# GpSimd's clearing between scatters: 8 columns in place of 384, and behind more of the scatters

## The reference

```
x = x + layernorm(linear_attention(layernorm(x)))     # 16 heads of 8, scan over the 256 rows
x = x + layernorm(moe(layernorm(x)))

moe(x) = shared(x) + sum over the two best of 8 experts of gate_e(x) * expert_e(x)
shared, expert_e: 128 -> 512 -> 128, gelu (tanh form) between, biases on both layers
gates: softmax of x @ Wr, the best two kept and scaled to the sum 1
```

## Time and profile before

| | us |
|---|---|
| three runs, median | 385.13 |
| lowest, highest | 382.33, 385.97 |
| the profiled execution | 381.27 |
| its span, first to last instruction | 379.4 |
| mean granted TensorE clock | 0.967 |

### The profile page before, as it was taken

One profiled execution on the slowest core, in us unless ns is written; L12 is line 12 of the kernel. 1 busy time (PEld: TensorE's weight loads), 2 busy tenths in 40 slices (PEclk: granted clock), 3 DMA queues, 4 the chain that ended last, 5 costly groups with the idle time before them and its releaser, 6 DMA issues.

```text
span 379.4 us, 8176 instructions
## 1 busy us (share of the span) xinstructions
PE 336.1 (89%) x2497; PEld 291.0 (77%) x2497; DVE 288.4 (76%) x688; ACT 256.8 (68%) x692; POOL 290.6 (77%) x393
## 2 busy tenths in 40 slices
PE   7869896999899898998799998999998699989891
PEld 3538485797786867877598898889997699989871
DVE  4998999799899999899966467745543359687667
ACT  3958874896896887867426884466552477587674
POOL 8778799478888687888778888888888667776640
PEclk9979997999999999999999999999998899999997
DMA  6576766566382606125059569979874589987417
GB/s 188 164 208 182 179 167 125 114 199 156 113 225 76 177 31 182 48 90 156 30 168 278 147 181 268 263 239 282 263 244 147 165 267 383 314 243 246 125 56 204
DMA packets 53522, 69.18 MB, mean 182 GB/s; under 512 B 6365, under 2 KB 37386, under 8 KB 53482
## 3 DMA queue, kind: packets, MB, share of 16 engines
q1 hardware_dynamic: 47556, 58.58, 54.5%
q0 software_dynamic: 4544, 9.35, 7.3%
q10 hardware_dynamic: 1382, 0.79, 0.8%
HBM read 40.06 MB, written 18.15 MB: 153 GB/s over the span
## 4 chain that ended last, share of the span: by engine, by line
PE 29%; DVE 16%; issue 8%; ACT 7%; POOL 7%; another core or an unknown queue 2%; DVEq 0%; ACTq 0%; POOLq 0%
PE bO L1551 8%; PE bS L1551 6%; POOL expert_lists L708 4%; DVE KV L1702 3%; ACT hs L1154 2%; PE bV L1526 2%; PE bV L1524 2%; PE bV L1525 2%; DVE KV L1693 1%; DVE Z L1710 1%; PE bO L1335 1%; DVE X L1625 1%; PE bA L1524 1%; DVE w_lo L2125 1%
## 5 line engine op out<-in xcount | busy, mean ns | idle before, releaser
L831 POOL DMA_INDIRECT expert_results<-yb,yrow x78 | 78.7, 1009 | 29.5 <-issue 19.3
L708 POOL DMA_INDIRECT expert_lists<-rows,pos x64 | 64.3, 1005 | 19.4 <-issue 17.2
L1702 DVE TENSOR_TENSOR_SCAN KV<-bS,KV 128x1024 f32<-128x1024 bf16 x32 | 72.7, 2276 | 0.3
L1335 PEld LDWEIGHTS bO<-wout_rot,Z 128*128 128x128 f32 x512 | 60.6, 192 | 8.4 <-POOL Z L790 5.1
L1335 PE MATMUL bO<-wout_rot,Z 128*128 128x128 f32 x512 | 63.2, 277 | 2.1 <-POOL Z L790 1.8
L2149 DVE COPY yrow<-xb 128x2 int32<-128x2 int32 x24 | 7.7, 321 | 42.3 <-remote 18.7
L1154 ACT ACTIVATE hs<-bV,KV 128x256 f32<-128x256 f32 x56 | 22.0, 477 | 18.9 <-PE bV L1526 10.4
L1551 PE MATMUL bO<-KV,hs 128*128 128x128 f32 x232 | 30.5, 286 | 3.7 <-ACT hs L1154 2.3
L1551 PEld LDWEIGHTS bO<-KV,hs 128*128 128x128 f32 x232 | 28.5, 199 | 5.1 <-ACT hs L1154 3.2
L1305 PE MATMUL bA<-w2s_sb,hs 128*128 128x128 f32 x224 | 28.8, 277 | 0.0
L734 POOL TENSOR_TENSOR KV<-shared,vr 128x1024 f32<-128x1024 f32 x10 | 23.6, 2363 | 5.7 <-ACT shared L995 5.4
(11 more groups left out here) (370 smaller groups left out, 995.9 us busy)
## 6 DMA issues: line engine op xcount, KB each, us to landing
KV<-packed_weights SPq DMA_DIRECT2D x21, 578.0 KB
Z<-packed_weights SPq DMA_DIRECT2D x18, 578.0 KB
xb<-expert_lists SPq DMA_DIRECT2D x39, 129.0 KB
vr<-vr SPq DMA_DIRECT2D x16, 224.0 KB, 2.5
shared<-expert_results SPq DMA_DIRECT2D x7, 512.0 KB
vr<-vr SPq DMA_DIRECT2D x16, 192.0 KB
vr<-vr SPq DMA_DIRECT2D x16, 160.0 KB
vr<-vr SPq DMA_DIRECT2D x16, 128.0 KB
```

The costliest lines, as they stand in the source:

```text
L708: g.indirect_dma_start(out=lists, out_offset=bass.IndirectOffsetOnAxis(ap=pos[:, m:m + 1], axis=0), in_=rows[:, m // TILES, m % TILES, :], ...
L831: g.indirect_dma_start(out=results, out_offset=bass.IndirectOffsetOnAxis(ap=yrow[n][:, c], axis=0), in_=yb[n][:, c, :], in_offset=None).th ...
L1335: ins = t.matmul(bO[:, j * D:(j + 1) * D], Z[:, d, j * P:(j + 1) * P], wout_rot[:, d], start=False, stop=True, skip_group_check=True)
L1702: v.tensor_tensor_scan(w, ps_keep, w, 0.0, ALU.mult, ALU.add).then_inc(s["kv_sum"], 1)
```

## The change

`spare` is 8 columns wide in place of 384, and `still()` stands behind both scatters of every block up to block 35 (NB - HALVED = 36), not only of the first. The list scatters have it where they had it. There are then 20 + 72 = 92 of them. Nothing else is changed: the same scatters in the same order, with the same semaphores.

```diff
-        spare = sb("spare", [P, 3 * P])
+        spare = sb("spare", [P, 8])
...
             AT_END = 4
-            PAIRED = 27
-            SINGLE = 2 * NBUF
...
                         in_=yb[n][:, c, :], in_offset=None).then_inc(blk_scat[n], 16)
-                    if b < SINGLE or b < PAIRED and c == 0:
+                    if b < NB - HALVED:
                         still()
```

## The result

The changed kernel takes 395.36 us, median of 4 runs (394.26 to 397.71), where the kernel before took 385.29 beside it: a ratio of 1.030, 95% interval 1.026 to 1.034. The forecast was 383.7. It is slower, by 10 us, and near the 393.4 of the rival of a second slow stretch. The profiled execution has a span of 394.7 us at a mean granted clock of 0.957. It is 15.3 us longer than the profiled one of the kernel before, which was 1% faster than its median, so differences between the two traces add up to more than the 10 us.

A forecast was written before the change was run, and what follows sets the result against it. TensorE was taken to set the pace from 251 us on. Of 19.5 us leaving GpSimd's queue, 0.55 + 0.82 = 1.4 us were to reach the path: ratio 0.9964, 383.7 us from 385.13, 8-in-10 range 376 to 388.5.

The forecast's parts named there:

- the rival of a second slow stretch: GpSimd 7 us ahead, scatters meet other loads, TensorE's results come late: 393.4 us, or 388.6 for half; chance 0.12.
- what the change takes out of GpSimd: 59 clearings each 0.33 us cheaper, so 19.5 us leave GpSimd's queue.
- both rivals: Old slow stretch gone or much smaller, chance 0.22; a second slow stretch, chance 0.12.
- Width: An 8-column clearing on GpSimd takes 0.10 us (bounds 0 and 0.21), so a scatter's period becomes 1.24 us.
- The 33 added ones: Added clearings between scatters 1.26 us apart cost nothing; 3.3 us in all if the idle time stays 0.30.
- (a) The second norm: Line 622, behind five clearings, starts at 210.4 in place of 210.94 us: gain 0.55 us, bounds 0 and 1.65.
- (b) Block 2: Block 2 scattered from about 236 us, 7 us sooner; VectorE's buffer wait at block 8 goes: gain 0.82 us, bounds 0 and 2.0.
- (c): SP's 4.6 us wait before loading block 13 goes, as list scatters land sooner; worth nothing on the path.
- The traffic: From 224 to 242 us three more scatters on full DMA engines could delay weights by 0.7 us; put at nothing.
- the old slow stretch: From 284 to 304 us three blocks take 9.7 us too much; the forecast left it in place.
- The other rival: Clearings behind both scatters remove the old slow stretch: 374.0 us if whole, 378.8 for half; chance 0.22.

The follow-up runs named there:

- e13: Kernel before with the 15 second clearings of blocks 12 to 26 back, 384 columns wide: 382.57 us, ratio 0.997.
- e2: Changed kernel with clearings of 384 columns at all 92 places: 380.65 us, ratio 0.992.
- e10: The changed kernel run again, unchanged, on another chip: ratio 1.031 to the kernel before.
- e15: Changed kernel with 512 columns behind lists and blocks 0 to 5, 256 for blocks 6 to 26, none after: 389.34 us, ratio 1.010.
- e16: Changed kernel with clearings of 512 columns at all 92 places: 390.78 us, ratio 1.015.
- e4: Changed kernel with one power of 128x1 elements on GpSimd in place of each clearing: 407.2 us, ratio 1.059.
- e18: The changed kernel run again, unchanged, beside e16 and e17: 394.93 us, ratio 1.025.
- e7: Changed kernel with 768 columns behind every second scatter only, none behind the first: 381.31 us, ratio 1.023.
- e5: Changed kernel with clearings of 256 columns at all 92 places: 376.38 us, ratio 1.006.
- e17: Changed kernel with 256 columns at all 92 places, as e5 but on another chip: 390.36 us, ratio 1.014.

## Why the prediction was wrong

**The step that failed** is the first of "what the change takes out of GpSimd": the clearing was priced as GpSimd's time alone, and taken for a pure cost since nothing reads `spare`. Its narrowing shortened the pause behind a scatter from 0.60 to 0.30 us, and with it TensorE's signals came up to 10.3 us late in place of 2.1 from 213 to 251 us: the program was living on the time that the clearing takes. Signs of it were in the trace before. ScalarE's 7.29 us in the earlier trace rows, which I took for a late sight of a result, is mostly not that, for the piece it waits for ended at 296.03 us, only 0.85 before. It is TensorE that was late, behind a held result of VectorE's in the same stretch, under single clearings, 5.5 us after its layer ended:

```profile
283.80 1.84 PE L1551 MATMUL bS<-KV,hs 128*128 128x128 f32 x15
```
```profile
291.13 0.17 DVE L2149 COPY yrow<-xb 128x2 int32<-128x2 int32 x1 [5.56 <-remote]
```

I wrote that the profile doesn't show what holds TensorE's results back, and put both rivals that hang on it at 0.34 together. Laying GpSimd's rows beside such waits would have given a hint: in the kernel before too, a row of list scatters without a clearing ends at 200.7 us, and VectorE is let go at 201.6.

**Width.** 0.12 us measured, 0.10 taken, within the bounds. The period is 1.27 us and not 1.24, as the idle time is 0.18. The 33 added ones cost nothing: 1.27 against 1.26. These terms were right and don't matter.

**(a) The second norm** was to gain 0.55 us. Line 622 starts at 211.98 us, 1.04 later than in the earlier trace rows. It starts 0.08 us behind the squares, so GpSimd no longer delays it, as forecast (0.2 to 0.3 us were given for it); but the squares themselves are late, behind ScalarE's 4.54 us for a held result.

**(b) Block 2** was to be scattered from 236 us on. It is 243.46, later than the 242.67 of the earlier trace rows: the queue stood 4.80 us for block 1's `yb`, which was itself held. So GpSimd's lead couldn't grow past the next `yb`. The wait of 2.61 us at 248.79 us was also misread: the landing was there at 247.93, and what came last, at 248.76, was TensorE's signal, 2.0 us late. It was a held result, and buffers played little part in it. **(c)** SP's wait at line 464 is gone, and is worth nothing, as said.

**The traffic.** The long waits end on TensorE's signals and not on the loads that were feared to land late, and the DMA share in the worst windows is 0.28 and 0.42. The statement of the Trainium skill (DMA: Bandwidth & Descriptors, Issuing engines are not separate DMA queues) that I weighed bears on bandwidth, and here there was bandwidth to spare; no run here shows it to matter.

**The rival that came true** had the right shape (results of TensorE late, TensorE idle and at the lower clock) and its threshold is half right: 9.62 and 12.22 us are more than the one block of 3.42 and cost over half of their length, but e13's 1 to 3.3 us each aren't free, as I had them, and cost a fifth of theirs. Its cause isn't what the runs point to: it made the loads that the scatters meet the reason, but results are held behind rows of close scatters long before GpSimd has any lead (ScalarE waits 3.13 us until 95.8 us in the kernel before). Its size came near by luck, by two errors that cancel: the new passages cost 20.8 us, not 9.7, and the old slow stretch, which I let stand, gave some 8 back. **The other rival**, that the slow stretch goes with paired clearings, was right for clearings of full width (e2, e13). Against it I held that shorter waits stand under paired ones; that is true too, and fits with its being worth only 1 to 4 us and not 9.7.

## What to carry to other kernels

An instruction whose output nobody reads may be there for the time it takes: before it is made cheaper, look at what other engines wait for while its neighbours run close together. When an engine waits for a result whose producer ended microseconds ago, lay every other engine's rows beside the end of that wait and look for the row that ends with it. A pause has a price as well (here 92 times the width, paid when the last wave reads back), so on the chips that hold results the best of the tried values lies between: 384 columns behind every scatter gave 0.992 and 0.993, 512 gave 1.015, 8 gave 1.025 to 1.031. On the chip that holds none, 512 columns gave 1.040 and 256 gave 1.006.

## What the runs showed of the hardware

- While GpSimd issued indirect scatters of 128 rows 0.30 us apart, VectorE and ScalarE waited up to 12.7 us at a time for results of TensorE, whose signals came up to 11.1 us late (e10). With 0.71 us behind each scatter the latest came 1.6 and 1.1 us late (e15, e16), with 0.8 us 0.1 (e4).
- From 205 to 260 us no signal of VectorE, ScalarE or GpSimd was over 0.04 us late in any of the 20 traces. Only TensorE's were, and held ones often came in bursts, 0.04 to 0.13 us apart.
- With 0.60 us the held results of e13 from 253 to 275 us are seen in step with GpSimd's cycle of 1.57 us, seven of ten at the end of a clearing, to 0.07 us.
- Late in a row of twelve scatters TensorE too stands between matmuls of one layer, up to 1.8 us at a time (1.9 in e18, 1.1 in e10), without a wait that the profile shows.
- Chips differ: the kernel before takes 385.1, 384.2 and 384.0 us on three and 374.0 on a fourth, where no result is held with pauses of 0.49 us and more, nor between the close pairs of e7. e5 there and e17 elsewhere are the same program: held 0 and 34.2 us from 213 to 251.
- One power of 128x1 elements takes 0.60 us on GpSimd, a memset of 8 columns 0.12 us, one of 512 columns 0.54 us.
